# A two-layer graph network on one core: the second gather of a tile adds onto the first one's rows

## The reference

```python
h = relu(layernorm(x))
nodes_i, nodes_j = h[src], h[dst]
m = mlp3(concat([nodes_i, nodes_j, edge_attr_64]))        # 320 -> 256 -> 256 -> 128, relu between
summed = segment_sum(m, src) + segment_sum(m, dst)
attention = differences of nodes of neighbouring blocks of 32
x = x + mlp3(concat([h, summed, attention]))              # 384 -> 256 -> 256 -> 128
```

## Time and profile before

| what | value |
|---|---|
| median of 3 runs | 889.4 us (889.25, 889.40, 904.84) |
| span of the profiled execution, first to last instruction | 779.9 us |
| outside the span, by the median | 109.5 us |
| PE busy | 754.1 us, 97% |
| DVE busy | 690.5 us, 89% |
| POOL busy | 554.3 us, 71% |
| ACT busy | 483.5 us, 62% |
| mean granted TensorE clock | 0.992 |

### The profile page before, as it was taken

How to read it: one execution, slowest core, us unless ns; L and a number is a source line. 1 busy time by engine, 2 the same in 40 slices (tenths; PEclk the granted TensorE clock), 3 DMA queues, 4 the chain that set the end, 5 groups by cost and what they waited for, 6 DMA issues and landing times.

```text
span 779.9 us, 13149 instructions
## 1 busy us (share of the span) xinstructions
PE 754.1 (97%) x4171; PEld 587.2 (75%) x4171; DVE 690.5 (89%) x1441; ACT 483.5 (62%) x646; POOL 554.3 (71%) x533
## 2 busy tenths in 40 slices
PE   7589999999999999999999999999999999999996
PEld 7467877778777877778777877778777877778755
DVE  7769999999999999999999999999999999999875
ACT  3255676666766667666766667666766667666723
POOL 3777777777777777777777777777777777777100
PEclk9799999999999999999999999999999999999999
DMA  8434434344434444334333443344333444343000
GB/s 230 143 120 122 128 122 122 114 124 125 123 111 123 124 125 124 110 122 129 122 112 118 127 125 122 110 123 127 122 116 116 128 122 123 114 123 101 1 1 27
DMA packets 42564, 90.13 MB, mean 116 GB/s; under 512 B 11136, under 2 KB 17920, under 8 KB 42496
## 3 DMA queue, kind: packets, MB, share of 16 engines
q0 software_dynamic: 24576, 67.14, 28.5%
q1 hardware_dynamic: 17920, 22.16, 9.4%
HBM read 86.64 MB, written 2.62 MB: 114 GB/s over the span
## 4 chain that ended last, share of the span: by engine, by line
PE 89%; POOL 4%; DVE 3%; issue 2%; DMA 1%; ACT 1%; DVEq 0%; SPq 0%; POOLq 0%
PE bank L614 29%; PE bank L593 22%; PE bank L603 14%; PE bank L575 8%; PE bank L581 8%; PE bank L624 4%; POOL tab_sb L436 2%; POOL tab_sb L444 2%; PE bank L699 1%; DVE ring L968 1%; PE bank L744 1%; PE bank L505 1%; DMA table_a<-tab_sb 1%; PE bank L707 0%; PE bank L693 0%
## 5 line engine op out<-in xcount | busy, mean ns | idle before, releaser
L436 POOL DMA_INDIRECT tab_sb<-table_a,ends_i x256 | 281.4, 1099 | 83.4 <-issue 77.7
L444 POOL DMA_INDIRECT tab_sb<-table_b,ends_i x256 | 260.0, 1016 | 78.0 <-issue 78.0
L968 DVE TENSOR_SCALAR ring<-dist,half_gap,times 128x1026 fp32r<-128x1026 f16 (+1 forms) x256 | 276.4, 1081 | 24.1 <-ACT dist L791 20.7
L791 ACT ACTIVATE dist<-iota_h,neg_mid 128x1026 f16<-128x1026 f16 (+1 forms) x256 | 292.6, 1144 | 0.0
L781 ACT ACTIVATE h_sb<-bank,b_sb 128x512 f32<-128x512 f32 x128 | 87.4, 683 | 189.8 <-PE bank L593 189.8
L614 PE MATMUL bank<-ring,m_hi 128*128 128x512 f32 x512 | 171.2, 415 | 1.3 <-DVE ring L968 1.1
L614 PE MATMUL bank<-ring,m_lo 128*128 128x512 f32 x512 | 161.0, 395 | 0.0
L593 PE MATMUL bank<-ring,w_hi 128*128 128x512 f32 x512 | 151.7, 398 | 1.4 <-DVE ring L948 1.4
L1017 DVE TENSOR_SCALAR oh_key<-iota_h,key_f,minus_base 128x258 bf16<-128x258 f16 x321 | 128.0, 399 | 0.0
L603 PE MATMUL bank<-w_sb,h_sb 128*128 128x128 f32 x1024 | 124.8, 275 | 0.0
L603 PEld LDWEIGHTS bank<-w_sb,h_sb 128*128 128x128 f32 x1024 | 119.5, 192 | 0.1
(11 more groups left out here) (176 smaller groups left out, 456.1 us busy)
## 6 DMA issues: line engine op xcount, KB each, us to landing
e_raw<-edge_attr_t SPq DMA_DIRECT2D x128, 128.0 KB, 3.0
tab_sb<-table_a,ends_i POOLq DMA_INDIRECT x256, 2.9
tab_sb<-table_b,ends_i POOLq DMA_INDIRECT x256, 2.9
table_a<-tab_sb SPq DMA_DIRECT2D x4, 256.0 KB, 3.7
table_b<-tab_sb SPq DMA_DIRECT2D x4, 256.0 KB, 2.8
x_sb<-x SPq DMA_DIRECT2D x2, 256.0 KB, 3.2
w_sb<-mW SPq DMA_DIRECT2D x2, 256.0 KB, 5.2
out<-oh_key SPq DMA_DIRECT2D x4, 128.0 KB, 1.8
```

Of the source, the lines that this page charges most:

```text
L436: nc.gpsimd.indirect_dma_start(got[:, b, t, 0, :], None, table_a, bass.IndirectOffsetOnAxis(ap=ends_i[:, 0, tile:tile + 1], axis=0),).then ...
L444: nc.gpsimd.indirect_dma_start(got[:, b, t, 1, :], None, table_b, bass.IndirectOffsetOnAxis(ap=ends_i[:, 1, tile:tile + 1], axis=0),).then ...
L791: nc.scalar.activation(to, of, ACT.Abs, bias=neg_mid[:, bass.ds(g * GT + t, 1)]).then_inc(dist_ready, 1)
L968: nc.vector.tensor_scalar(to, of, half_gap[:, tile], times[:, tile], ALU.is_equal, ALU.mult).then_inc(inc_ready, 1)
```

## The change

- The gather of `table_b` (now `add_b`) writes to the same slot as the gather of `table_a` and adds its rows to what lies there while they move (`compute_op=ALU.add`). It therefore waits until the first gather has landed (`ga_done`).
- `add_pairs` on VectorE is gone. TensorE waits on `rows_added` of each tile itself, four waits a group in place of two.
- The slot that is now free makes `got` four buffers deep: group g uses buffer g % 2 and slot g // 2 % 2. GpSimd waits for group g-4 in place of g-2.
- In a group the four gathers of `table_a` are issued first and then the four adding ones, where they alternated.

```diff
+    SLOTS = 4
...
-        gb_done = [[sem(f"gb_done{b}_{j}") for j in range(GT)] for b in range(2)]
-        pair_added = sem("pair_added")
+        rows_added = [[sem(f"rows_added{b}_{j}") for j in range(GT)] for b in range(2)]
...
                 nc.gpsimd.indirect_dma_start(
-                    got[:, b, t, 0, :], None, table_a,
+                    got[:, b, t, g // 2 % 2, :], None, table_a,
                     bass.IndirectOffsetOnAxis(ap=ends_i[:, 0, tile:tile + 1], axis=0),
                 ).then_inc(ga_done[b][t], 16)
 
-            def gather_b(g, t):
+            def add_b(g, t):
 
                 b, tile = g % 2, g * GT + t
+                pool.wait_ge(ga_done[b][t], 16 * (g // 2 + 1))
                 nc.gpsimd.indirect_dma_start(
-                    got[:, b, t, 1, :], None, table_b,
+                    got[:, b, t, g // 2 % 2, :], None, table_b,
                     bass.IndirectOffsetOnAxis(ap=ends_i[:, 1, tile:tile + 1], axis=0),
-                ).then_inc(gb_done[b][t], 16)
-
-            for t in range(GT):
-                gather_a(0, t)
-            pool.wait_ge(tab_b_stored, 16 * NC // 2)
-            for t in range(GT):
-                gather_b(0, t)
-            for g in range(1, GROUPS):
-                if g >= 2:
-                    pool.wait_ge(z1t_psum, KH * (g - 1))
+                    compute_op=ALU.add,
+                ).then_inc(rows_added[b][t], 16)
+
+            for g in range(GROUPS):
+                if g >= SLOTS:
+                    pool.wait_ge(z1t_psum, KH * (g - SLOTS + 1))
                 for t in range(GT):
                     gather_a(g, t)
-                    gather_b(g, t)
+                if g == 0:
+                    pool.wait_ge(tab_b_stored, 16 * NC // 2)
+                for t in range(GT):
+                    add_b(g, t)
...
                 for t in range(GT):
-                    if k == 0 and t % 2 == 0:
-
-                        pe.wait_ge(pair_added, 2 * g + (t // 2 + 1))
-                    mm = nc.tensor.matmul(z1t_bank[k][:, t * P:(t + 1) * P], got[:, b, t, 0, part], ident[:, :],
+                    if k == 0:
+                        pe.wait_ge(rows_added[b][t], 16 * (n + 1))
+                    mm = nc.tensor.matmul(z1t_bank[k][:, t * P:(t + 1) * P], got[:, b, t, n % 2, part], ident[:, :],
                                           start=False, stop=True, is_transpose=True, skip_group_check=True)
...
-                if nxt:
-                    add_pairs(g + 1, 1 - b, i + b)
```

More of the change, by code:

```diff
@@ L999, in group @@
                     window_sums(i)
[L1001 to L1009, removed]
             def window_tile(w):
```

## The result

The changed kernel takes 900.9 us (median of 20 runs, 898.1 to 903.6). The kernel before, in runs on the same chip, takes 898.0 us (20 runs, 889.3 to 910.3). The ratio is 1.0047, 95% interval 1.0025 to 1.0069: slower by a little, and certainly not by 2%. Some executions of each kernel take over 1.5% more than its fastest one; all ratios leave them out, the medians don't. The profiled execution of the changed kernel took 900.9 us with a span of 899.2.

A forecast was written before the change was run, and what follows sets the result against it. The prediction took PE to be the bound at 10.94 us a group, GpSimd close behind at 10.89. Loop 0, start -1.6, behind the loop 0 took the median 889.4 to 888 us; range 885 to 970, own case 886 to 907.

The forecast's parts named there:

- The adding gather, X = 0.95: GpSimd's issue time X for one adding gather, taken equal to the plain gather's 0.95 us; group 10.25 us, price 0.
- The break-even: Issue time of the adding gather, 1.12 us, at which GpSimd's group equals PE's 10.94 us.
- the ends 0.94 and 1.89: Limits for the adding gather's issue time on GpSimd: 0.94 us like a plain one, 1.89 if all its work doubled.
- PE stays the bound at 10.94 us a group: In the loop PE, busy without a pause, sets 10.94 us a group before and after the change; loop change 0.
- rival 1: GpSimd becomes the bound because X is above 1.12 us; 965 us at X = 1.42, chance 0.38.
- GpSimd's group, 6.45 + 4X: GpSimd's time in us for a group's eight gathers: issue, four plain gathers, 0.27 stretch and four adding ones.
- The additions: Removing VectorE's 128 additions (82.6 us) gains 0 on PE's loop path; GpSimd's gathers lose 0.63 us a group of stretch.
- The wait in front of the adding gather: GpSimd's wait for the first gather's landing before the adding one: price 0, with 2.1 us of cover.
- Order and slots, 0: First gathers ahead of adding ones and four slots give 0; PE's two extra waits a group, at most 4 us, taken as 0.
- The start, -1.6 us: Before the loop, group 3's transposes on PE start at about 64.7 us in place of 66.28, a gain of 1.6 us.
- Rival 2: The DMA engines or their landing become the bound; without overlap 14.3 us a group, +215 us, 1100 us, chance 0.07.
- Rival 4: Nothing shifts: PE's start waits end on landings 1.6 us later; 889 us, inside the forecast's case, which together has chance 0.52.

The follow-up runs named there:

- the second profile: The kernel before, unchanged, profiled again: 906.3 us, ratio 0.9999, profiled span 901.8 us.
- four unread gathers: Four plain gathers a group into a tensor nobody reads, added to the changed kernel with two slots and no second gather (774.6 us): 886.8 us, 0.989.
- ordered landings from another queue: Changed kernel with two slots and no second gather, plus four plain 128 KB loads of table_b a group from SyncE: 774.8 us, 0.852.
- TensorE's order changed: Kernel before with scatter 1 of the group before moved ahead of messages: 891.7 us, 0.984; with scatter 1 and 2 moved: 982.7 us.

## Why the prediction was wrong

The direction was missed by little and the time by 13 us, but that the time came so near is chance: two errors of about 120 us cancelled, a price that was put at nothing and a loss of the kernel before that its first profile doesn't show.

- **The adding gather, X = 0.95.** This choice carried the forecast, and it is the first step that failed. X is 1.59 (1.54 at the least). The break-even was rightly at 1.12, the ends 0.94 and 1.89 hold the value, and it lies nearer to the upper one. "The same 128 rows and indices" was the wrong reason: GpSimd's time for them grows by 0.6 us. The Trainium skill ("Collectives: The Full Stack", the bandwidth ceiling) says that an add needs two read descriptors where a copy needs one. The traces count packets and engine time, not descriptors: an adding gather has 144 packets where a plain one has 48, and takes 0.93 us of each DMA engine ((0.387 x 899.2 - 256 x 0.43) / 256) where a plain one takes 0.43. Twice the engine time fits the rule. The other page of the Trainium skill ("DMA: Bandwidth & Descriptors", anatomy of one DMA) calls descriptor generation a small part. GpSimd's time to issue a gather is no small part here but the whole bound; how much of it is the descriptors, no row tells.
- **PE stays the bound at 10.94 us a group.** This step failed too, and before any change: the first profile shows a kernel that the timed runs don't. In a profile like the timed runs the group lasts 12.8 us, with TensorE's signals late. The run with plain second gathers tests it: it is the changed kernel with X = 0.99, well below 1.12, and took 922.5 us. So with X as it was taken the forecast would have failed too. The warning was on the table: a median 109.5 us above the span. It was called time outside the span in place of a doubt about the profile. Added to a base of 889.4, rival 1 with X = 1.59 would have given 1009 us; added to the span of 779.9 it gives the measured 899.2.
- **GpSimd's group, 6.45 + 4X.** Held: 12.81 worked out, 12.77 measured.
- **The additions.** Held where it can be seen: they freed nothing on TensorE's path, and plain first gathers fell from 1099 to 991 ns in the mean, 27.8 us / 64 = 0.43 us a group, where 0.63 was expected (from the second profile's 1058 ns it is 17.1 us / 64 = 0.27). The removal on VectorE was not tried by itself.
- **The wait in front of the adding gather.** Held at 0: no gather of GpSimd waited for a landing.
- **Order and slots, 0.** Held: 1.000 for the order, and with two buffers 0.999, no worse than with four slots.
- **The start, -1.6 us.** Failed as a consequence of X. The landing is 3.7 us where 2.9 was counted, and the last transposes of group 3, at 66.28 before, start at 74.76 (start, duration, idle time before):

```profile
74.76 0.33 PE L580 MATMUL bank<-ident,tab_sb 128*128 128x128 f32 x1 [1.60 <-DMA tab_sb<-table_b,ends_i]
```

- **Rival 1** named the mechanism and each of its marks: transposes that wait for the landing, GpSimd without a wait to the end (its last gather ends at 838.5), the chain over the gathers. Its price of 76 us was for X = 1.42. **Rival 2** fell: the gathers' queue has 38.7% of the engines, and the landing grew by 0.8 us; its 0.9 us of engine time for an adding gather was right. **Rival 4**'s number, no shift, is near the result for a reason that it didn't have.

Shown: in the changed kernel GpSimd's issuing is the bound, since it never waits and an adding gather takes 0.6 us more of it; no run shows the kernel faster without that price, because the other loss then comes back. Shown too: four unread gathers more bring the time from 774.6 to 886.8 us, 0.989 of the kernel before, with rows of 512 bytes as of 1 KB, and neither a busy GpSimd, nor the order, nor ordered landings from another queue do it. Argued only: that TensorE's late signals are the way in which this happens. With 4, 6, 7 and 8 gathers they grow (2, 62, 151 and 194 us) and the time follows once they outlast TensorE's other work. But with TensorE's order changed, relus are late by 245 us in a kernel that is faster, and by 182 in one that is slower. Open: why gathers make them late, and why the execution of the first profile was free of it.

## What to carry to other kernels

If the timed runs are 14% above the profile's span, profile again before costing anything; a base that the timed runs don't have makes every sum wrong. On a queue within a few tenths of a us of being the bound, measure the new instruction's issue time first: here the price of the add in flight was the time of the engine that issues it, not of the DMA engines. A mix (two adding gathers of four, 0.969) can beat both pure versions (1.00 and 1.005), so it is worth a run, even if its reason is open as it is here. And a label in a wait table has a limit of its own: with six gathers relus were late by 62 us, of which the "remote" row shows 2.3.

## What the hardware showed that was not expected

- An accumulating indirect DMA of 128 rows of 1 KB takes 1.54 us of GpSimd at the least and 1.59 in the mean, where a plain one beside it takes 0.94 and 0.99. Its landing takes 3.7 us in place of 2.9, its packets are 144 in place of 48, and its time on each DMA engine is 0.93 us in place of 0.43.
- With 6, 7 and 8 indirect DMAs in a group of 11 to 12.6 us, ScalarE saw TensorE's semaphores late: 36, 59 and 63 of 128 relus by over 1 us (1.9, 9.8 and 5.1 us at the most), and the time was 782.7, 829.2 and 886.8 us. With four it was one relu, and 774.6 us. Rows of 512 bytes do it as those of 1 KB do (61 relus). In the changed kernel, with eight, no relu_second was late; the copies of the messages were (41 of 64, by 92 us).
- The granted clock hardly takes part in the series of unread gathers: 0.984 with eight and 0.993 with six, a difference of 1% beside 13% of time. In the kernel before it is 0.96, with TensorE busy for 793.0 us in place of 754.1, so the clock may hold up to 39 of the 122 us there; no run tells what part.
- Iotas on GpSimd stretched VectorE's one-hot instructions (L1017 in the kernel before) from 402 to 630 ns in the mean, and cost next to nothing (777.0 us), since VectorE was not the bound.
